# The reciprocals of a Sinkhorn iteration made by GpSimd, as powers of minus one, instead of by VectorE

## The chip, the cores and the metric

One core of one Trainium2 chip runs the kernel. The metric is the device time of one launch in microseconds (us). Three runs of the kernel before gave 2599.68, 2599.71 and 2604.77 us; the median is 2599.71.

## What is computed

The input `x` has 16 batches of 256 tokens by 2048 numbers. Each batch goes through a linear attention (with keys and values from a context of the same shape) and then through a mixing block. The mixing block works per token on four streams of 512 numbers and needs a doubly stochastic 4x4 matrix for every token, which 50 rounds of Sinkhorn normalisation make:

```python
def step(carry, _):
    u, v = carry
    u = -jax.nn.logsumexp(Z + v[..., None, :], axis=-1)
    v = -jax.nn.logsumexp(Z + u[..., :, None], axis=-2)
    return ((u, v), None)
(u, v), _ = jax.lax.scan(step, (u0, v0), None, length=num_iters)   # 50
return jnp.exp(Z + u[..., :, None] + v[..., None, :])
...
x = x + attention(layernorm(x), ctx_4096, ctx_4096, ...)
x = x + mix(layernorm(x), ...)     # H_res = sinkhorn_log(...) in it
```

## The kernel before

Everything runs in f32. For each of the 16 batches the kernel walks a list of **places**: 16 "A" places and 16 "B" places (key logits, their exponentials, the key-value context), and 27 "Q" places (query logits, softmax, attention out, the return of the rows). Each of the five engines has its own program, which walks the same list in order and issues its share of a place, in a fixed order, with semaphore waits. So the order on each engine is written out by hand, and no scheduler changes it.

**The Q places.** Query tiles are handled in pairs, one pair in two places. For a pair VectorE subtracts the maxima (L943, L953), ScalarE takes exponentials (L1260), GpSimd adds the halves of each head (L1501, `query_half`), VectorE sums and inverts (L961, L965, `query_sum`), GpSimd multiplies (L1509, `query_normalise`). Some places later, VectorE floors a norm (L973), GpSimd raises it to the power -0.5 (L1519), VectorE scales the attention output (L983, `scale_pair`), and GpSimd adds it to the rows (L1526, `add_pair`). GpSimd also makes the low halves of the next context (L1480) and of x (L1484), and weight matrices for the mixing (L1491).

**The Sinkhorn iteration.** The 4x4 matrices of several batches are worked on together. `GROUPS = (4, 4, 4, 2, 2)` gives the batches of each of five groups; a batch has two tiles of 128 tokens, so T, the tiles of a group, is 8, 8, 8, 4 and 4. Each round is run as scalings of a matrix `skp`: a **step** is a product with the last scale (L1062 or L1058, 128 x 16T), a sum over rows or columns (L1063 or L1059, 16T to 4T numbers) and a reciprocal (L1064 or L1060, 128 x 4T). After at most 10 rounds ScalarE's logarithms refresh u and v. There are 98 such steps with a reciprocal in a group, among 116 pieces in all. Each of VectorE's small instructions waits for the one before it through `s_skd` (`step`).

The pieces are laid over the places of the batches that follow the group. A batch has 31 places that may take pieces: 16 among the A and B places, and Q5 to Q19. The first two groups have four batches to do it in, so one piece a place. Groups 2 (T = 8) and 3 (T = 4) have two batches each, so nearly every place takes two pieces. The last group, T = 4, is run in the tail, after the last batch. VectorE's and ScalarE's programs each keep a generator (`sinkhorn`) that goes one piece further at each "sink" task.

Of the kernel before, what the change touches and what calls it, by code (L numbers as in the profile page):

```python
# [5 lines left out]
ALU = mybir.AluOpType  # L6
# [30 lines left out]
def xattn_ffn(nc, x, ctx, ctx_t, x_t, wq_t, wk_t, wv_t, wo_t, bo, g, w_maps_t, base, gate, w_branch, streams, coef_rows, bias_rows, out):  # L37
# [212 lines left out]
    with stack:  # L250
        def sb(name, shape, dt=F32):
            return stack.enter_context(nc.sbuf_tensor(name, shape, dt))

        def sem(name):
            return stack.enter_context(nc.semaphore(name))
# [167 lines left out]
        def wait_read(w, n):  # L423
# [6 lines left out]

        SK_ACTS = 5 + 3 * -(-(SINKHORN_ITERS - 1) // REFRESH) + 1
        CONSTS = 11
        SK_STEPS = 3 + 1 + 4 + 1 + 3 + sum(
            6 * min(REFRESH, SINKHORN_ITERS - d) - 1 + 4 for d in range(1, SINKHORN_ITERS, REFRESH)) + 6 + 5

        def sync_program(e):
# [77 lines left out]
            def store_coefs(gr):  # L514
                tokens = slice(FIRST[gr] * C, (FIRST[gr] + GROUPS[gr]) * C)
                T = GROUPS[gr] * CT
                w.wait_ge(s_skd, (gr + 1) * SK_STEPS)
                if gr:
                    for i in range(2):
                        w.wait_ge(s_coef[i], gr * 16)  # L520
                nc.sync.dma_start(coef_rows[tokens].rearrange("(t p) s i -> p t s i", p=P), coef_all[:, 0:T]).then_inc(
                    s_coef[0], 16)
                nc.sync.dma_start(bias_rows[tokens].rearrange("(t p) i -> p t i", p=P), bias_all[:, 0:T]).then_inc(
                    s_coef[1], 16)
# [285 lines left out]
        def vector_program(e):  # L810
# [184 lines left out]
            def step(instruction):  # L995

                instruction.then_inc(s_skd, 1)
                skd[0] += 1
                w.wait_ge(s_skd, skd[0])

            def sinkhorn(gr):
# [9 lines left out]
                def over_j(v):  # L1011
                    return v.unsqueeze(2).broadcast_to([P, T, STREAMS, STREAMS])
# [7 lines left out]
                def over_streams(v):  # L1020
                    return v.unsqueeze(2).broadcast_to([P, T, STREAMS])

                w.wait_ge(s_lg, first + GROUPS[gr])
                if gr:
                    for i in range(2):
# [27 lines left out]
                while done < SINKHORN_ITERS:  # L1053
                    w.wait_ge(s_ska, acts)
                    rounds = min(REFRESH, SINKHORN_ITERS - done)
                    for r in range(rounds):
                        if r:
                            step(nc.vector.tensor_tensor(skw, skp, over_j(skb), ALU.mult))  # L1058
                        step(nc.vector.tensor_reduce(skr, skw if r else skp, AX_X, ALU.add))  # L1059
                        step(nc.vector.reciprocal(ska, skr))  # L1060
                        yield
                        step(nc.vector.tensor_tensor(skw, skp, over_i(ska), ALU.mult))  # L1062
                        step(nc.vector.tensor_reduce(skr, by_column(skw), AX_X, ALU.add))  # L1063
                        step(nc.vector.reciprocal(skb, skr))  # L1064
                        yield
                    done += rounds
                    w.wait_ge(s_ska, acts + 1)
                    step(nc.vector.tensor_tensor(sku, sku, skr, ALU.add))
                    yield
                    w.wait_ge(s_ska, acts + 2)  # L1070
                    step(nc.vector.tensor_tensor(skv, skv, skr, ALU.add))
                    step(nc.vector.tensor_tensor(skw, skz, over_i(sku), ALU.add))
                    step(nc.vector.tensor_tensor(skw, skw, over_j(skv), ALU.add))
                    yield
                    acts += 3
# [161 lines left out]
        def scalar_program(e):  # L1237
# [86 lines left out]

            def own_first(k):
                ct, i = k // STREAMS, k % STREAMS
                w.wait_ge(s_skd, len(GROUPS) * SK_STEPS)
                nc.scalar.activation(own[k], x_sb[(NB - 1) % 2][:, ct, quarter(0)], ACT.Identity,
                                     bias=bias_all[:, own_tile + ct, i:i + 1],
                                     scale=coef_all[:, own_tile + ct, 0, i:i + 1]).then_inc(s_first, 1)  # L1330

            def sinkhorn(gr):
                T = GROUPS[gr] * CT
                skp, skw, ska, skb, skr = (a[:, 0:T] for a in (skp_all, skw_all, ska_all, skb_all, skr_all))
                post = coef_all[:, 0:T, STREAMS, :]

                def function(target, source, func, count):
                    w.wait_ge(s_skd, count)
                    nc.scalar.activation(target, source, func).then_inc(s_ska, 1)

                d = gr * SK_STEPS + 3
# [12 lines left out]
                function(skp, skw, ACT.Exp, d)  # L1354
                yield
                done = 1
                while done < SINKHORN_ITERS:
                    rounds = min(REFRESH, SINKHORN_ITERS - done)
                    done += rounds
                    d += 6 * rounds - 1  # L1360
                    for _ in range(2 * rounds - 1):
                        yield
                    function(skr, ska, ACT.Ln, d)
# [83 lines left out]
        def pool_program(e):  # L1447
# [10 lines left out]
            nc.gpsimd.memset(chain_t, 1.0).then_inc(s_const, 1)  # L1458
            w.wait_ge(s_const, 6)
            nc.gpsimd.memset(half_power[:], -0.5).then_inc(s_const, 1)  # L1460
            w.wait_ge(s_const, 7)

            nc.gpsimd.memset(mix_mask[:], 1.0).then_inc(s_const, 1)
# [57 lines left out]
            def add_pair(b, p):  # L1521
# [110 lines left out]
```

## Time and profile before

| | |
|---|---|
| median of three runs | 2599.71 us |
| the profiled execution's own time | 2600.5 us |
| its span, first to last instruction | 2598.8 us |
| TensorE matmul busy | 2422.8 us (93%) |
| VectorE busy | 1764.0 us (68%) |
| ScalarE busy | 1168.1 us (45%) |
| GpSimd busy | 1068.3 us (41%) |

The busy times are sums over the whole span; a matmul's end is modelled, so 93% says that TensorE had work issued nearly always, not that it ran at its peak. The time of the launch is 1.7 us more than the span. Batches 1 to 3 have no Sinkhorn pieces in them, batches 4 to 11 have one in each of their 31 places, batches 12 to 15 two. From batch 7 on, most batches also carry matmuls of the mixing of finished groups.

### The profile page before, as it was taken

The page shows a single profiled execution, that of the slowest core. Times are in us where ns is not written, and L with a number is a line of the kernel's source. Part 1 is how long each engine was busy: PE and PEld are TensorE (multiplying, and loading weights), DVE is VectorE, ACT ScalarE, POOL GpSimd, SP SyncE. Part 2 cuts the span into 40 slices and gives each one's busy share as a digit, 9 for nine tenths or more (in the row PEclk, how much of TensorE's full clock was granted, in tenths as well). Part 3 has the DMA queues.
Part 4 walks back from the last instruction along what each step waited for, and adds up shares of the span by engine and source line. Part 5 has one row for each costly group of instructions (what it writes and reads, how often), then busy time and mean ns, then how long its engine had stood idle before and what let it go on. Part 6 is the DMA issues. An engine that isn't in the chain of part 4 may idle for free.

```text
span 2598.8 us, 35329 instructions
## 1 busy us (share of the span) xinstructions
PE 2422.8 (93%) x12004; PEld 1920.9 (74%) x12004; DVE 1764.0 (68%) x4242; ACT 1168.1 (45%) x2439; POOL 1068.3 (41%) x979
## 2 busy tenths in 40 slices
PE   7999999999999999999999999999999999999864
PEld 6887878787888787777877778777776776777521
DVE  3554645456877777666766768776688786967787
ACT  3454444445453444446454444535445344443332
POOL 1534536271635345362634527262362442624410
PEclk9999999999999999999999999999999999999877
DMA  7112222313123122225334330323424423331265
GB/s 234 49 66 98 73 91 71 99 40 100 60 67 101 57 98 74 89 72 156 98 122 138 97 125 33 105 75 112 127 65 123 132 84 116 98 117 45 80 184 164
DMA packets 200145, 255.72 MB, mean 98 GB/s; under 512 B 43550, under 2 KB 109854, under 8 KB 199966
## 3 DMA queue, kind: packets, MB, share of 16 engines
q1 hardware_dynamic: 199966, 253.47, 31.1%
q8 instruction: 96, 1.57, 0.3%
q14 instruction: 83, 0.68, 0.1%
HBM read 177.53 MB, written 75.89 MB: 98 GB/s over the span
## 4 chain that ended last, share of the span: by engine, by line
PE 64%; DVE 21%; POOL 6%; issue 6%; ACT 3%; DMA 1%; SPq 0%; DVEq 0%; POOLq 0%; ACTq 0%
PE kc_bank L641 15%; PE big L700 10%; PE tb L742 4%; PE big L615 4%; PE tb L627 4%; PE big L617 3%; PE big L616 3%; PE tb L756 3%; PE big L674 3%; PE big L676 3%; PE big L675 3%; PE tb L685 2%; PE misc L722 2%; DVE stats L883 2%; POOL x_tr L1526 2%
## 5 line engine op out<-in xcount | busy, mean ns | idle before, releaser
L1255 ACT COPY turned<-tb 128x512 f32<-128x512 f32 x512 | 298.7, 587 | 754.4 <-PE tb L685 481.6
L700 PE MATMUL big<-merged,turned 128*128 128x256 f32 x2048 | 494.6, 385 | 32.8 <-ACT turned L1255 26.0
L641 PE MATMUL kc_bank<-ctxt,turned 128*128 128x256 f32 x2048 | 480.7, 381 | 0.0
L700 PEld LDWEIGHTS big<-merged,turned 128*128 128x128 f32 x2048 | 386.2, 191 | 107.9 <-ACT turned L1255 22.5
L641 PEld LDWEIGHTS kc_bank<-ctxt,turned 128*128 128x128 f32 x2048 | 376.0, 191 | 53.4 <-issue 10.8
L1484 POOL TENSOR_TENSOR in_l<-x_sb,in_h 128x512 fp32r<-128x512 f32 x128 | 168.7, 1344 | 589.8 <-ACT in_h L1295 589.8
L1509 POOL TENSOR_TENSOR q_sb<-q_sb,qsum 128x1024 f32<-128x1024 f32 x128 | 243.8, 1905 | 281.6 <-DVE qsum L965 281.5
L674 PE MATMUL big<-wq_h,in_h 128*128 128x512 f32 x512 | 238.3, 465 | 16.9 <-DVE q_sb L953 16.4
L856 DVE TENSOR_REDUCE kmax<-big 128x1 f32<-128x512 f32 x256 | 172.3, 685 | 106.3 <-PE big L617 103.5
L615 PE MATMUL big<-in_h,wk_h 128*128 128x512 f32 x512 | 238.0, 465 | 6.4 <-ACT k_exp L1246 6.1
L756 PE MATMUL tb<-mix_ld,mix_w 121*96 121x512 f32 (+2 forms) x324 | 188.9, 680 | 56.4 <-DVE mix_w L1134 26.3
L943 DVE TENSOR_REDUCE qmax<-big 128x8 f32<-128x512 f32 x256 | 175.9, 687 | 86.8 <-PE big L676 82.8
L617 PE MATMUL big<-in_h,wk_l 128*128 128x512 f32 x512 | 203.7, 398 | 0.0
L616 PE MATMUL big<-in_l,wk_h 128*128 128x512 f32 x512 | 203.4, 397 | 0.0
L676 PE MATMUL big<-wq_h,in_l 128*128 128x512 f32 x512 | 203.1, 397 | 0.0
L675 PE MATMUL big<-wq_l,in_h 128*128 128x512 f32 x512 | 202.8, 396 | 0.0
L1246 ACT ACTIVATE k_exp<-big,kmax 128x512 f32<-128x512 f32 x256 | 175.3, 689 | 49.8 <-DVE kmax L863 49.6
L1501 POOL TENSOR_TENSOR x_pre<-q_sb 128x512 f32<-128x512 f32 x128 | 162.8, 1272 | 76.3 <-ACT q_sb L1260 76.2
L1323 ACT COPY mix_out<-tb 96x512 f32<-96x512 f32 (+2 forms) x162 | 93.9, 580 | 219.5 <-PE tb L756 192.5
L973 DVE TENSOR_SCALAR nrm<-nrm 128x2 f32<-128x2 f32 x128 | 111.4, 870 | 104.4 <-ACT squares L1271 104.0
L1260 ACT ACTIVATE q_sb<-q_sb 128x1024 f32<-128x1024 f32 x128 | 135.6, 1060 | 103.3 <-DVE q_sb L953 103.3
L878 DVE TENSOR_SCALAR on<-kc_bank,ksum 128x256 f32<-128x256 f32 x64 | 31.0, 484 | 222.3 <-PE kc_bank L641 219.8
(148 smaller groups left out, 4490.0 us busy)
## 6 DMA issues: line engine op xcount, KB each, us to landing
mix_ld<-streams SPq DMA_DIRECT2D x157, 240.0 KB
ctxt<-in_ctx_t SPq DMA_DIRECT2D x64, 512.0 KB, 4.3
x_sb<-in_x SPq DMA_DIRECT2D x64, 512.0 KB, 6.2
x_tr<-in_x_t SPq DMA_DIRECT2D x64, 512.0 KB, 6.7
streams<-x_sb SPq DMA_DIRECT2D x64, 512.0 KB, 3.1
stage<-in_ctx SPq DMA_DIRECT2D x60, 512.0 KB, 4.1
out<-mix_out SPq DMA_DIRECT2D x157, 192.0 KB, 2.2
streams<-y_sb SPq DMA_DIRECT2D x32, 256.0 KB, 2.0
```

The lines of the kernel that those rows point to most:

```text
L615: nc.tensor.matmul(big[i], wk_h[:, ct, cols], in_h[:, ct, quarter(i)], start=ct == 0, stop=False)
L616: nc.tensor.matmul(big[i], wk_h[:, ct, cols], in_l[:, ct, quarter(i)], start=False, stop=False)
L617: t = nc.tensor.matmul(big[i], wk_l[:, ct, cols], in_h[:, ct, quarter(i)], start=False, stop=ct == CT - 1)
L641: t = nc.tensor.matmul(kc_bank[:, 0:C], turned[n % 3][:, j * P:(j + 1) * P], ctxt[:, nt, :], start=nt == 0, stop=nt == NT - 1)
L674: nc.tensor.matmul(big[i % 2], in_h[:, ct, at], wq_h[:, ct, :], start=ct == 0, stop=False)
L675: nc.tensor.matmul(big[i % 2], in_h[:, ct, at], wq_l[:, ct, :], start=False, stop=False)
L676: t = nc.tensor.matmul(big[i % 2], in_l[:, ct, at], wq_h[:, ct, :], start=False, stop=ct == CT - 1)
L700: t = nc.tensor.matmul(big[2 + p % 2][:, half], turned[n % 3][:, dt * P:(dt + 1) * P], merged[:, dt, :], start=dt == 0, stop=dt == DT - 1)
L756: t = nc.tensor.matmul(bank[0:count * STREAMS, :], weights, mix_ld[k][0:ONES + 1, :], start=True, stop=True)
L943: nc.vector.tensor_reduce(qmax[:, i % 2, :], big[i % 2].rearrange(heads, d=DIM_HEAD), AX_X, ALU.max).then_inc(s_qmax, 1)
L1255: nc.scalar.copy(turned[k % 3][:], tb[n % 2][:]).then_inc(s_tba, 1)
L1509: nc.gpsimd.tensor_tensor(exps, exps, qsum[:, p % 2, 1, :].unsqueeze(2).broadcast_to([P, 2 * HEADS, DIM_HEAD]), ALU.mult).then_inc(s_qn, 1)
```

## The change

For all groups but the last, VectorE's reciprocal of each step is dropped. GpSimd's program gets a generator of its own which, at the same "sink" task, waits for the sum (`s_skd`) and writes `skr ** -1` as a TENSOR_TENSOR of 128 x 4T with the operation `pow` and a tile of minus ones; `s_ski` counts these. VectorE's next product waits for `s_ski`, and so does ScalarE's logarithm at a refresh. The counts of `s_skd` are adapted everywhere (`sk_steps`).

```diff
+                def reciprocal(target):
+
+                    if gr == LAST:
+                        step(nc.vector.reciprocal(target, skr))
+
+                def inverted():
+                    if gr < LAST:
+                        halves[0] += 1
+                        w.wait_ge(s_ski, halves[0])
+
...
                         if r:
+                            inverted()
                             step(nc.vector.tensor_tensor(skw, skp, over_j(skb), ALU.mult))
                         step(nc.vector.tensor_reduce(skr, skw if r else skp, AX_X, ALU.add))
-                        step(nc.vector.reciprocal(ska, skr))
+                        reciprocal(ska)
                         yield
+                        inverted()
                         step(nc.vector.tensor_tensor(skw, skp, over_i(ska), ALU.mult))
                         step(nc.vector.tensor_reduce(skr, by_column(skw), AX_X, ALU.add))
-                        step(nc.vector.reciprocal(skb, skr))
+                        reciprocal(skb)
                         yield
...
+            def sinkhorn(gr):
+                T = GROUPS[gr] * CT
+                ska, skb, skr = (a[:, 0:T] for a in (ska_all, skb_all, skr_all))
+                w.wait_ge(s_minus, 1)
+                for _ in range(5):
+                    yield
+                d = sum(map(sk_steps, range(gr))) + 12
+                done = 1
+                while done < SINKHORN_ITERS:
+                    rounds = min(REFRESH, SINKHORN_ITERS - done)
+                    done += rounds
+                    for r in range(rounds):
+                        d += 2 if r else 1
+                        w.wait_ge(s_skd, d)
+                        nc.gpsimd.tensor_tensor(ska, skr, minus_one[:, 0:T], ALU.pow).then_inc(s_ski, 1)
+                        yield
+                        d += 2
+                        w.wait_ge(s_skd, d)
+                        nc.gpsimd.tensor_tensor(skb, skr, minus_one[:, 0:T], ALU.pow).then_inc(s_ski, 1)
+                        yield
+                    d += 4
+                    yield
+                    yield
+
             def behind(place):
                 for task in tasks.get(place, ()):
                     b = task[1]
+                    if task[0] == "sink" and b < LAST:
+                        if b not in running:
+                            running[b] = sinkhorn(b)
+                        next(running[b], None)
```

What stands on GpSimd in two Q places of a batch of group 0, before (L1519 the power of the norm, L1501 the half sums, L1509 the normalisation, L1526 the rows):

```order
L1519 TENSOR_TENSOR nrm<-nrm,half_power 128x2
L1501 TENSOR_TENSOR x_pre<-q_sb 128x512
L1509 TENSOR_TENSOR q_sb<-q_sb,qsum 128x1024
L1526 TENSOR_TENSOR x_tr<-x_tr,on 128x512
L1480 TENSOR_TENSOR in_l<-stage,in_h 128x512
L1519 TENSOR_TENSOR nrm<-nrm,half_power 128x2
```

And in the same places after the change (the same four are L1547, L1529, L1537 and L1554 there, the context's low half is L1508, and L1570 and L1574 are the new powers):

```order
L1547 TENSOR_TENSOR nrm<-nrm,half_power 128x2
L1529 TENSOR_TENSOR x_pre<-q_sb 128x512
L1570 TENSOR_TENSOR ska<-skr,minus_one 128x32
L1537 TENSOR_TENSOR q_sb<-q_sb,qsum 128x1024
L1554 TENSOR_TENSOR x_tr<-x_tr,on 128x512
L1508 TENSOR_TENSOR in_l<-stage,in_h 128x512
L1574 TENSOR_TENSOR skb<-skr,minus_one 128x32
L1547 TENSOR_TENSOR nrm<-nrm,half_power 128x2
```

One power stands ahead of the normalisation, the other between the rows' addition and the power of the norm.

On VectorE in the same two places, before (L1062 and L1063, L1058 and L1059 are a step's product and sum):

```order
L943 TENSOR_REDUCE qmax<-big 128x8
L961 TENSOR_REDUCE qsum<-x_pre 128x16
L965 RECIPROCAL qsum<-qsum 128x16
L953 TENSOR_TENSOR q_sb<-big,qmax 128x512
L973 TENSOR_SCALAR nrm<-nrm 128x2
L1062 TENSOR_TENSOR skw<-skp,ska 128x128
L1063 TENSOR_REDUCE skr<-skw 128x32
L1064 RECIPROCAL skb<-skr 128x32
L943 TENSOR_REDUCE qmax<-big 128x8
L953 TENSOR_TENSOR q_sb<-big,qmax 128x512
L983 SCALAR_TENSOR_TENSOR on<-big,nrm,g_rows 128x256 x2
L1058 TENSOR_TENSOR skw<-skp,skb 128x128
```

And after (L952, L970, L974, L962, L982, L992 are the query's instructions, L1085 and L1086, L1080 and L1081 the steps'):

```order
L952 TENSOR_REDUCE qmax<-big 128x8
L970 TENSOR_REDUCE qsum<-x_pre 128x16
L974 RECIPROCAL qsum<-qsum 128x16
L962 TENSOR_TENSOR q_sb<-big,qmax 128x512
L982 TENSOR_SCALAR nrm<-nrm 128x2
L1085 TENSOR_TENSOR skw<-skp,ska 128x128
L1086 TENSOR_REDUCE skr<-skw 128x32
L952 TENSOR_REDUCE qmax<-big 128x8
L962 TENSOR_TENSOR q_sb<-big,qmax 128x512
L992 SCALAR_TENSOR_TENSOR on<-big,nrm,g_rows 128x256 x2
L1080 TENSOR_TENSOR skw<-skp,skb 128x128
L1081 TENSOR_REDUCE skr<-skw 128x32
```

Only the reciprocal of the step is gone; all else keeps its place. In a batch of group 2, with two pieces a place, two powers stand together on GpSimd after the change:

```order
L1537 TENSOR_TENSOR q_sb<-q_sb,qsum 128x1024
L1554 TENSOR_TENSOR x_tr<-x_tr,on 128x512
L1508 TENSOR_TENSOR in_l<-stage,in_h 128x512
L1574 TENSOR_TENSOR skb<-skr,minus_one 128x32
L1570 TENSOR_TENSOR ska<-skr,minus_one 128x32
L1547 TENSOR_TENSOR nrm<-nrm,half_power 128x2
L1529 TENSOR_TENSOR x_pre<-q_sb 128x512
L1508 TENSOR_TENSOR in_l<-stage,in_h 128x512
L1574 TENSOR_TENSOR skb<-skr,minus_one 128x32
L1570 TENSOR_TENSOR ska<-skr,minus_one 128x32
```

Before, the same stretch had none of the L1570 and L1574 rows; the second of two waits for VectorE's product and sum, which wait for the first.

## Rows read from the trace of the kernel before

**Rows 1.** The page's first part: busy time, share of span, instructions.

```profile
PE 2422.8 (93%) x12004; PEld 1920.9 (74%) x12004; DVE 1764.0 (68%) x4242; ACT 1168.1 (45%) x2439; POOL 1068.3 (41%) x979
```

**Rows 2.** Busy time by stretch: batch 1, batch 5, batch 12, the tail.

```profile
181.13:322.06 140.93, 138.17 (x731) 115.53 (x730) 73.84 (x159) 65.57 (x135) 63.99 (x51) 1.00 0.24 79
748.49:892.91 144.42, 139.23 (x730) 115.41 (x729) 107.30 (x249) 66.32 (x138) 64.00 (x52) 1.00 0.23 77
1801.93:1974.85 172.92, 159.68 (x765) 123.08 (x763) 135.83 (x326) 75.99 (x159) 69.16 (x69) 0.98 0.35 108
2457.04:2598.80 141.76, 78.33 (x124) 21.93 (x124) 108.53 (x392) 42.59 (x87) 15.05 (x41) 0.75 0.61 172
```

**Rows 3.** Timeline of GpSimd in batch 5: start us, duration us, instruction [idle before].

```profile
823.18 1.91 POOL L1509 TENSOR_TENSOR q_sb<-q_sb,qsum 128x1024 f32<-128x1024 f32 x1 [2.64 <-DVE qsum L965]
825.05 1.41 POOL L1526 TENSOR_TENSOR x_tr<-x_tr,on 128x512 f32<-128x512 f32 x1
826.42 1.27 POOL L1480 TENSOR_TENSOR in_l<-stage,in_h 128x512 fp32r<-128x512 f32 x1
827.65 0.70 POOL L1519 TENSOR_TENSOR nrm<-nrm,half_power 128x2 f32<-128x2 f32 x1
...
832.23 1.91 POOL L1509 TENSOR_TENSOR q_sb<-q_sb,qsum 128x1024 f32<-128x1024 f32 x1 [1.34 <-DVE qsum L965]
...
840.02 1.90 POOL L1509 TENSOR_TENSOR q_sb<-q_sb,qsum 128x1024 f32<-128x1024 f32 x1 [2.63 <-DVE qsum L965]
```

**Rows 4.** Timeline of VectorE in the same two places.

```profile
828.38 0.88 DVE L983 SCALAR_TENSOR_TENSOR on<-big,nrm,g_rows 128x256 f32<-128x256 f32 x2 [0.92 <-POOL nrm L1519]
829.18 0.56 DVE L1062 TENSOR_TENSOR skw<-skp,ska 128x128 f32<-128x128 f32 x1
829.77 0.39 DVE L1063 TENSOR_REDUCE skr<-skw 128x32 f32<-128x128 f32 x1
830.19 0.35 DVE L1064 RECIPROCAL skb<-skr 128x32 f32<-128x32 f32 x1
830.58 0.69 DVE L943 TENSOR_REDUCE qmax<-big 128x8 f32<-128x512 f32 x1
831.19 0.68 DVE L961 TENSOR_REDUCE qsum<-x_pre 128x16 f32<-128x512 f32 x1
831.90 0.25 DVE L965 RECIPROCAL qsum<-qsum 128x16 f32<-128x16 f32 x1
```

**Rows 5.** Groups of instructions by form: busy us, mean ns of one.

```profile
L1060 DVE RECIPROCAL ska<-skr 128x32 f32<-128x32 f32 x147 | 51.9, 353 | 5.1
...
L1501 POOL TENSOR_TENSOR x_pre<-q_sb 128x512 f32<-128x512 f32 x128 | 162.8, 1272 | 76.3 <-ACT q_sb L1260 76.2
L1519 POOL TENSOR_TENSOR nrm<-nrm,half_power 128x2 f32<-128x2 f32 x128 | 89.8, 701 | 66.7 <-DVE nrm L973 64.3
L1491 POOL TENSOR_TENSOR mix_w<-mix_mask,mix_co 120x96 f32<-120x96 f32 x151 | 53.8, 364 | 100.2 <-DMA mix_w<-bias_rows 100.2
```

**Rows 6.** Timeline of VectorE among the B places of batch 5.

```profile
750.29 0.29 DVE L1059 TENSOR_REDUCE skr<-skw 128x32 f32<-128x128 f32 x1
...
761.06 0.35 DVE L1060 RECIPROCAL ska<-skr 128x32 f32<-128x32 f32 x1
763.24 0.48 DVE L878 TENSOR_SCALAR on<-kc_bank,ksum 128x256 f32<-128x256 f32 x1 [1.83 <-PE kc_bank L641]
...
768.60 0.41 DVE L845 COPY on<-tb 128x256 f32<-128x256 f32 x1
...
771.89 0.69 DVE L856 TENSOR_REDUCE kmax<-big 128x1 f32<-128x512 f32 x1
...
782.13 0.35 DVE L1064 RECIPROCAL skb<-skr 128x32 f32<-128x32 f32 x1
```

**Rows 7.** Timeline of GpSimd in batch 12 (group 2) and batch 14 (group 3).

```profile
1895.06 1.90 POOL L1509 TENSOR_TENSOR q_sb<-q_sb,qsum 128x1024 f32<-128x1024 f32 x1 [6.45 <-DVE qsum L965]
...
1905.33 1.91 POOL L1509 TENSOR_TENSOR q_sb<-q_sb,qsum 128x1024 f32<-128x1024 f32 x1 [2.54 <-DVE qsum L965]
...
2234.87 1.91 POOL L1509 TENSOR_TENSOR q_sb<-q_sb,qsum 128x1024 f32<-128x1024 f32 x1 [3.26 <-DVE qsum L965]
...
2244.75 1.91 POOL L1509 TENSOR_TENSOR q_sb<-q_sb,qsum 128x1024 f32<-128x1024 f32 x1 [2.00 <-DVE qsum L965]
```

More of the change, by code:

```diff
@@ L317, in xattn_ffn @@
         s_skd = sem("s_skd")
+        s_minus = sem("s_minus")
+        s_ski = sem("s_ski")
         s_ska = sem("s_ska")
@@ L367, in xattn_ffn @@
         half_power = sb("half_power", [P, CT])
+        minus_one = sb("minus_one", [P, TMAX, STREAMS])
         neg_m2 = sb("neg_m2", [P, CT])
@@ L432, in xattn_ffn, with sk_steps @@
         CONSTS = 11
+        HALVES = 2 * (SINKHORN_ITERS - 1)
+        def sk_steps(gr):
+            return SK_STEPS - (HALVES if gr < LAST else 0)
         SK_STEPS = 3 + 1 + 4 + 1 + 3 + sum(
@@ L516, in store_coefs @@
                 T = GROUPS[gr] * CT
-                w.wait_ge(s_skd, (gr + 1) * SK_STEPS)
+                w.wait_ge(s_skd, sum(map(sk_steps, range(gr + 1))))
                 if gr:
@@ L1021, in over_streams @@
                     return v.unsqueeze(2).broadcast_to([P, T, STREAMS])
+                halves = [gr * HALVES]
+                def reciprocal(target):
[5 more added lines that the diff above has]
+                        w.wait_ge(s_ski, halves[0])
                 w.wait_ge(s_lg, first + GROUPS[gr])
@@ L1057, in sinkhorn @@
                         if r:
+                            inverted()
                             step(nc.vector.tensor_tensor(skw, skp, over_j(skb), ALU.mult))
                         step(nc.vector.tensor_reduce(skr, skw if r else skp, AX_X, ALU.add))
-                        step(nc.vector.reciprocal(ska, skr))
+                        reciprocal(ska)
                         yield
+                        inverted()
                         step(nc.vector.tensor_tensor(skw, skp, over_i(ska), ALU.mult))
                         step(nc.vector.tensor_reduce(skr, by_column(skw), AX_X, ALU.add))
-                        step(nc.vector.reciprocal(skb, skr))
+                        reciprocal(skb)
                         yield
                     done += rounds
+                    inverted()
                     w.wait_ge(s_ska, acts + 1)
@@ L1326, in own_first @@
                 ct, i = k // STREAMS, k % STREAMS
-                w.wait_ge(s_skd, len(GROUPS) * SK_STEPS)
+                w.wait_ge(s_skd, sum(map(sk_steps, range(len(GROUPS)))))
                 nc.scalar.activation(own[k], x_sb[(NB - 1) % 2][:, ct, quarter(0)], ACT.Identity,
@@ L1339, in function @@
                     nc.scalar.activation(target, source, func).then_inc(s_ska, 1)
-                d = gr * SK_STEPS + 3
+                d = sum(map(sk_steps, range(gr))) + 3
                 function(skp, skp, ACT.Exp, d)
@@ L1355, in sinkhorn @@
                 yield
-                done = 1
+                done, halves = 1, gr * HALVES
                 while done < SINKHORN_ITERS:
@@ L1359, in sinkhorn @@
                     done += rounds
-                    d += 6 * rounds - 1
+                    d += (6 if gr == LAST else 4) * rounds - 1
                     for _ in range(2 * rounds - 1):
                         yield
+                    if gr < LAST:
+                        halves += 2 * rounds
+                        w.wait_ge(s_ski, halves)
                     function(skr, ska, ACT.Ln, d)
@@ L1460, in pool_program @@
             nc.gpsimd.memset(half_power[:], -0.5).then_inc(s_const, 1)
+            nc.gpsimd.memset(minus_one[:], -1.0).then_inc(s_minus, 1)
             w.wait_ge(s_const, 7)
@@ L1526, in add_pair @@
                 nc.gpsimd.tensor_tensor(pair, pair, on[:], ALU.add).then_inc(s_sum, 1)
+            def sinkhorn(gr):
[21 more added lines that the diff above has]
+                    yield
+            running = {}
             def behind(place):
```

## The prediction

> **What bounds the kernel now.** I read the page's busy shares first, then the busy times of stretches, then the timelines of GpSimd and VectorE side by side, and last the groups by form for prices.
>
> The shares suggest room: GpSimd is busy 41% of the span, VectorE 68% [rows 1]. The stretches say how little VectorE's load costs. A batch without Sinkhorn pieces takes 140.93 us, with TensorE busy for 138.17; batch 5, with one piece a place, takes 144.42 although VectorE is busy 33 us more [rows 2]. So in the batches of groups 0 and 1 all the pieces together cost about 3.5 us a batch. Batch 12, with two pieces a place and mixing matmuls as well, takes 172.92.
>
> Where those few us go is seen in the timelines. Through the Q places runs a ring between GpSimd and VectorE. GpSimd normalises (L1509, 1.91), adds rows (L1526, 1.41), in every second pair makes a context half (L1480, 1.27), takes the power of the norm (L1519, 0.70) [rows 3]; VectorE waited 0.92 for exactly that power, scales (L983, 0.88), does the step (0.56, 0.39, 0.35), then L943, L961 and L965 (0.69, 0.68, 0.25) [rows 4], and L965 releases the next L1509. The sum is 9.1 us, and the ring took 9.05 (823.18 to 832.23); the next one, without a context half, took 7.79 (832.23 to 840.02) [rows 3]. The mean is 8.4. GpSimd's 41% is thus misleading: in the Q places it is half of what sets the pace.
>
> **The change part by part.** *Removed:* 3 x 98 reciprocals of 128x32 at 353 ns and 98 of 128x16. A step on VectorE goes from one start to the next in 0.39 us for the reciprocal (830.19 to 830.58 [rows 4]). Of a pair's two, one is in the ring; the other stands beside GpSimd's normalisation.
>
> *Added:* 392 powers on GpSimd. Their price, W, is the large unknown. The trace has powers of 128x2 only, 701 ns. GpSimd's products and sums take 1272 ns for 512 elements and 364 for 96 [rows 5], so 2.2 ns an element on a base of 0.155 us. Of the power's 0.70 us some 0.54 are therefore its own arithmetic, for two elements. If all of it is start-up, a 128x32 costs 0.70 + 30 x 0.0022 = 0.77 us and a 128x16 0.73. If all of it is paid per element (0.27 each), they cost 0.155 + 32 x 0.272 = 8.9 and 4.5 us. No row lies between. [...] Between ends a factor of twelve apart I take the geometric middle, 2.6 us for 128x32 and 1.8 for 128x16, and keep both ends.
>
> The Trainium skill, "GPSIMD Engine Reference", section 4.1, says to do elementwise work on VectorE, GpSimd being about 2x slower, and section 3.1 gives about 2.6 cycles per element for a two-input operation. By that count, as an estimate from the page, 30 more elements would add 0.065 us and the power would be at my lower end, with the sum at about 2677 us. The trace agrees for products (2.2 ns an element); for powers it shows only that two elements already cost far more than that [rows 5].
>
> *Ring, one piece a place.* By the order in the section on the change, the power of the odd place stands between the rows' addition and the power of the norm, so all of W enters the ring; the power of the even place runs beside L943, L961 and L965, which give 1.6 us of cover, and only W - 1.6 shows. With about 0.1 us for two handovers a pair becomes longer by W + 0.1 - 0.39 + max(0, W - 1.6): 0.48 us at the low end, 3.3 at 2.6, 15.9 at the high end. Of a batch's 31 places 15 are Q places; 98 of 116 pieces carry a power; that is 22 pairs a group, 44 for groups 0 and 1. Sum: +21, +146, +700 us. Queued behind the power on GpSimd are L1519 and the next L1509; VectorE's scaling waits for the one, TensorE's transposes for the other, so nothing hides it.
>
> *A and B places, one piece.* Here GpSimd is mostly idle. The 16 steps run from 750.29 to 782.48, 32.2 us or 2.0 each [rows 6]. After the change a step cannot repeat sooner than product and sum (0.67) + two handovers (0.17) + W: 1.6 us at the low end, 3.4 in the middle, 9.7 at the high. At the low end only the four steps that follow at 1.07 us in each run of B places get longer, partly in the idle 1.83 us in front of L878: I take +9 us in all. Otherwise 16 steps take 55 or 156 us instead of 32, so 1.43 or 7.7 us a step, for 2 x 54 steps: +154, +834.
>
> *Groups 2 and 3, two pieces a place.* Both powers of a place are in the chain, since the second waits for a product and a sum that wait for the first. The ring becomes 1.9 + 1.4 + 0.64 (half of L1480) + 0.7 + 0.87 + three times 0.67 + 0.5 of handovers = 8.0, + 3W + max(W, 1.6): 11.9, 18.4, 43.6 us, against 10.27 before [rows 7]. There are 11 such pairs in group 2: +18, +89, +366. In group 3 the steps are smaller (0.5), the base 7.5 and the powers 128x16: 11.3, 14.7, 25.5 against 9.88 [rows 7], +15, +53, +172. In their 27 A and B places with powers a place becomes two steps, one exposed power with its handovers, and the longer of the second power and 1.1 to 1.2 us of VectorE's other work (L856 0.69 and a chain instruction, as L845 0.41 [rows 6]): for T = 8 it goes from 3.3 (two steps of 1.07 and the other work) to 3.5, 6.9, 19.5 us (+5, +97, +437), for T = 4 from 2.8 to 3.1, 4.9, 10.3 (+8, +57, +203).
>
> *The rest:* the last group is as before; ScalarE's logarithms wait for `s_ski` where they waited for the reciprocal, within the W counted; one memset more at the start is hidden behind the first loads. Nothing moves on TensorE or the DMA queues.
>
> **The sum.** Low 21+9+18+15+5+8 = 76; middle 146+154+89+53+97+57 = 596; high 700+834+366+172+437+203 = 2712. On the profiled execution's 2600.5 us that is 2677, 3197 and 5312; the median of the runs stands 0.8 below that execution, which changes nothing here.
>
> **The rivals.**
> *A, the power is nearly all start-up* (W up to about 1.3 us): 2677 to 2830 us. For it: a product costs hardly more for more elements. Against: 0.54 us for two elements is long for a mere start.
> *B, the power is paid element by element* (W of 6 us and more for 128x32): 4300 to 5312 us. For it: the arithmetic must be done on every element, and nothing in the trace shows that it overlaps. Against: only that GpSimd's simple loop does overlap its elements.
> *C, VectorE's relief wins* (the other side). If W with its handovers were below 0.39 us, the ring and the two-piece places would only lose reciprocals: 44 x 0.39 = 17 us in the first ring, about 1.5 us for each of 22 pairs (33) and 0.7 us for each of 54 A and B places (38): 2600 - 88 = 2512 us. Against it stands the row of 128x2, already at 0.70 [rows 5]; it decides only below W = 0.3.
> *D, GpSimd's power fits everywhere in idle time*, since it is busy only 41%: then no change, 2600. Against: the ring, in which VectorE already waits for GpSimd [rows 4].
> One thing may add to the middle case: in the tail, where TensorE is busy 78.33 of 141.76 us, its granted clock is 0.75 [rows 2], a mix of its two levels (1.2 and 2.4 GHz). If TensorE waits for the ring and its clock falls for stretches of the batches, its 138 us of work a batch at 2.4 GHz would become the bound again. I don't add it; the range covers it.
>
> **How the numbers follow.** Middle, W from 1.3 to 6 us: chance 0.50, own range 2830 to 4300, time 3200. B 0.26; A 0.18; C 0.03; D 0.03. The range of 8 in 10 leaves out the edges of A and B, so 2690 to 5300; it is wide because one price is unknown by a factor of twelve and enters 392 times. A measurement of this kernel can tell about 0.2% from no change. Faster by more than that is C, 0.03; within it D, 0.03; slower 0.94.
>
> **What would show it.** In the profile after: the two lines of powers with their mean for 128x32 and 128x16 (W itself; the whole size of the result hangs on it); VectorE's products waiting for them; GpSimd's L1509 rows of batch 5 more than 8.4 us apart, at about 11.7 for W = 2.6; batches 1 to 3 still at 140.9 us and the tail of the last group unchanged. Per power, groups 2 and 3 should lose more than groups 0 and 1 at the same W. It would be wrong in mechanism if the powers are long and the batches keep their length, or if the lost time stands in front of instructions that neither GpSimd nor VectorE releases; wrong in size if W is far from 2.6.

## The result

| | before | after |
|---|---|---|
| median | 2599.69 us (4 runs, 2599.59 to 2604.77) | 4045.94 us (4 runs, 4045.14 to 4047.53) |
| ratio | | 1.555, interval 1.553 to 1.557 |

The kernel got slower by 1446 us. The forecast was slower, 3200 us, in a range of 2690 to 5300: the side and the range held, but the loss was 2.4 times the 596 us that the sum had. The range held because it was wide: it ran from a power of under 1 us to one of 8.9 us.

The page after begins so (shares of the span in brackets, against [rows 1]):

```profile
span 4044.5 us, 35511 instructions
...
PE 2801.9 (69%) x12004; PEld 2154.8 (53%) x12004; DVE 1700.6 (42%) x3850; ACT 1165.6 (29%) x2439; POOL 2926.7 (72%) x1372
```

VectorE's busy time fell by 63 us, although the 392 reciprocals that it no longer makes had taken 129 (353 and 253 ns each): the products of the steps (L1080 and L1085, before L1058 and L1062), which now often start beside a GpSimd product, took 295 us in all against 173, as the last section explains, and the scalar operation on the norm (L982, before L973) 55 against 111. GpSimd's busy time grew by 1858 us. The groups of GpSimd's instructions by form name the price (busy us, mean ns of one):

```profile
L1574 POOL TENSOR_TENSOR skb<-skr,minus_one 128x32 f32<-128x32 f32 x147 | 798.0, 5429 | 111.0 <-DVE skr L1086 111.0
L1570 POOL TENSOR_TENSOR ska<-skr,minus_one 128x32 f32<-128x32 f32 x147 | 798.0, 5429 | 143.2 <-DVE skr L1081 143.2
...
L1570 POOL TENSOR_TENSOR ska<-skr,minus_one 128x16 f32<-128x16 f32 x49 | 142.2, 2902 | 40.4 <-DVE skr L1081 40.4
...
L1547 POOL TENSOR_TENSOR nrm<-nrm,half_power 128x2 f32<-128x2 f32 x128 | 89.8, 702 | 46.6 <-DVE nrm L982 44.5
```

The three sizes lie on one line: 0.375 us and 0.158 us an element give 0.69, 2.90 and 5.43 us. A 128x32 power took 5.43 us where I had taken 2.6, between ends of 0.77 and 8.9.

The chain of work that ended last changed hands. The page before and the page after have, as shares of the span:

```profile
PE 64%; DVE 21%; POOL 6%; issue 6%; ACT 3%; DMA 1%; SPq 0%; DVEq 0%; POOLq 0%; ACTq 0%
POOL 53%; PE 25%; DVE 14%; issue 6%; ACT 2%; DMA 0%; SPq 0%; DVEq 0%; POOLq 0%; ACTq 0%
```

From batch 4 to batch 15, where the powers are, the chain after goes over the powers L1570 and L1574 for 1720 of 3299 us and over TensorE for 443.

By stretch the loss sits where the forecast put it (batches 1, 5, 12, 14; against [rows 2]):

```profile
180.34:321.24 140.90, 138.15 (x731) 115.54 (x730) 73.83 (x159) 65.51 (x135) 64.08 (x51) 1.00 0.24 79
858.03:1120.63 262.60, 170.22 (x730) 134.98 (x728) 106.30 (x219) 65.96 (x138) 219.38 (x81) 0.81 0.13 42
2578.90:3001.39 422.49, 210.25 (x775) 155.64 (x774) 122.05 (x275) 76.75 (x160) 355.18 (x121) 0.71 0.15 45
3381.17:3663.76 282.59, 187.69 (x768) 140.81 (x767) 112.59 (x277) 76.48 (x159) 223.82 (x123) 0.82 0.22 70
```

Batch 1, without Sinkhorn pieces, is where it was (140.90 against 140.93). Batch 5 went from 144.4 to 262.6, batch 12 from 172.9 to 422.5. The tail with the last group takes 142.1 us (3902.37 to the end) against 141.8.

The ring in the Q places of group 0, on GpSimd's timeline (start, duration; against [rows 3]):

```profile
733.76 1.90 POOL L1537 TENSOR_TENSOR q_sb<-q_sb,qsum 128x1024 f32<-128x1024 f32 x1
735.62 1.31 POOL L1554 TENSOR_TENSOR x_tr<-x_tr,on 128x512 f32<-128x512 f32 x1
736.89 1.27 POOL L1508 TENSOR_TENSOR in_l<-stage,in_h 128x512 fp32r<-128x512 f32 x1
738.11 5.44 POOL L1574 TENSOR_TENSOR skb<-skr,minus_one 128x32 f32<-128x32 f32 x1
743.52 0.69 POOL L1547 TENSOR_TENSOR nrm<-nrm,half_power 128x2 f32<-128x2 f32 x1
744.18 1.25 POOL L1529 TENSOR_TENSOR x_pre<-q_sb 128x512 f32<-128x512 f32 x1
745.39 1.31 POOL L1508 TENSOR_TENSOR in_l<-stage,in_h 128x512 fp32r<-128x512 f32 x1
746.67 5.43 POOL L1570 TENSOR_TENSOR ska<-skr,minus_one 128x32 f32<-128x32 f32 x1
752.07 1.90 POOL L1537 TENSOR_TENSOR q_sb<-q_sb,qsum 128x1024 f32<-128x1024 f32 x1
...
763.07 5.44 POOL L1570 TENSOR_TENSOR ska<-skr,minus_one 128x32 f32<-128x32 f32 x1 [0.55 <-DVE skr L1081]
768.48 1.90 POOL L1537 TENSOR_TENSOR q_sb<-q_sb,qsum 128x1024 f32<-128x1024 f32 x1
```

GpSimd has no gap from 733.76 to 752.07: in the pair with context halves its own queue sets the time. In the next pair it waits once, 0.55 us for VectorE's sum at 763.07. A pair takes 18.31 us with context halves and 16.41 without, 17.36 in the mean; 8.4 plus the prediction's W + 0.1 - 0.39 + (W - 1.6) at W = 5.43 is 17.4. On VectorE's timeline of the same places the waits stand in brackets:

```profile
733.82 1.98 DVE L1085 TENSOR_TENSOR skw<-skp,ska 128x128 f32<-128x128 f32 x1 [3.33 <-POOL ska L1570]
...
744.25 0.88 DVE L992 SCALAR_TENSOR_TENSOR on<-big,nrm,g_rows 128x256 f32<-128x256 f32 x2 [6.58 <-POOL nrm L1547]
...
747.97 0.15 DVE L982 TENSOR_SCALAR nrm<-nrm 128x2 f32<-128x2 f32 x1
752.13 1.99 DVE L1085 TENSOR_TENSOR skw<-skp,ska 128x128 f32<-128x128 f32 x1 [4.01 <-POOL ska L1570]
```

The longest wait is not for the reciprocal itself but for the power of the norm (L1547), queued behind a power of the iteration. Among the A and B places GpSimd's powers follow one another with little between them but the handovers and VectorE's product and sum:

```profile
859.52 5.43 POOL L1570 TENSOR_TENSOR ska<-skr,minus_one 128x32 f32<-128x32 f32 x1 [0.80 <-DVE skr L1081]
865.76 5.43 POOL L1574 TENSOR_TENSOR skb<-skr,minus_one 128x32 f32<-128x32 f32 x1 [0.81 <-DVE skr L1086]
871.91 5.43 POOL L1570 TENSOR_TENSOR ska<-skr,minus_one 128x32 f32<-128x32 f32 x1 [0.73 <-DVE skr L1081]
```

That is 6.2 us a step; the formula's 0.67 + 0.17 + W is 6.27. From 908 us on in the same batch a GpSimd product (L1512) runs between the powers, VectorE's product beside it takes 1.3 us, and a step takes 7.2. And with two pieces a place (batch 12) both powers are exposed:

```profile
2774.03 5.43 POOL L1570 TENSOR_TENSOR ska<-skr,minus_one 128x32 f32<-128x32 f32 x1 [0.79 <-DVE skr L1081]
2779.43 1.90 POOL L1537 TENSOR_TENSOR q_sb<-q_sb,qsum 128x1024 f32<-128x1024 f32 x1
2781.96 5.42 POOL L1574 TENSOR_TENSOR skb<-skr,minus_one 128x32 f32<-128x32 f32 x1 [0.64 <-DVE skr L1086]
2788.18 5.42 POOL L1570 TENSOR_TENSOR ska<-skr,minus_one 128x32 f32<-128x32 f32 x1 [0.79 <-DVE skr L1081]
2793.57 0.69 POOL L1547 TENSOR_TENSOR nrm<-nrm,half_power 128x2 f32<-128x2 f32 x1
...
2808.05 1.95 POOL L1537 TENSOR_TENSOR q_sb<-q_sb,qsum 128x1024 f32<-128x1024 f32 x1
```

From 2779.43 to 2808.05 the pair takes 28.6 us; the formula 8.0 + 4W gives 29.7.

### The profile page after: what moved, and what is told of

Same layout as the page of the kernel before. It is cut to its first block, busy times and chain, and to the rows that moved or that the text cites. A ratio compares the mean times of both kernels' runs of the same rounds, so it can differ in the third digit from the quotient of the medians.

```text
span 4044.5 us, 35511 instructions
## 1 busy us (share of the span) xinstructions
PE 2801.9 (69%) x12004; PEld 2154.8 (53%) x12004; DVE 1700.6 (42%) x3850; ACT 1165.6 (29%) x2439; POOL 2926.7 (72%) x1372
## 4 chain that ended last, share of the span: by engine, by line
POOL 53%; PE 25%; DVE 14%; issue 6%; ACT 2%; DMA 0%; SPq 0%; DVEq 0%; POOLq 0%; ACTq 0%
POOL skb L1574 22%; POOL ska L1570 21%; PE kc_bank L650 6%; PE big L709 4%; POOL q_sb L1537 3%; DVE skw L1085 2%; DVE skw L1080 2%; PE big L624 2%; POOL x_pre L1529 2%; POOL x_tr L1554 2%; POOL in_l L1508 2%; PE big L626 2%; PE big L625 2%; DVE skr L1086 1%; DVE stats L892 1%
## 5 line engine op out<-in xcount | busy, mean ns | idle before, releaser
L1570 POOL TENSOR_TENSOR ska<-skr,minus_one 128x32 f32<-128x32 f32 (+1 forms) x196 | 940.2, 4797 | 183.7 <-DVE skr L1081 183.7
L1574 POOL TENSOR_TENSOR skb<-skr,minus_one 128x32 f32<-128x32 f32 (+1 forms) x196 | 940.2, 4797 | 138.3 <-DVE skr L1086 138.3
L709 PE MATMUL big<-merged,turned 128*128 128x256 f32 x2048 | 594.7, 442 | 276.8 <-DVE on L992 220.3
L709 PEld LDWEIGHTS big<-merged,turned 128*128 128x128 f32 x2048 | 445.5, 222 | 396.0 <-DVE on L992 274.6
L650 PE MATMUL kc_bank<-ctxt,turned 128*128 128x256 f32 x2048 | 539.6, 415 | 2.3 <-ACT turned L1279 2.3
L1085 DVE TENSOR_TENSOR skw<-skp,ska 128x128 f32<-128x128 f32 (+1 forms) x245 | 160.6, 656 | 665.4 <-POOL ska L1570 663.8
L1080 DVE TENSOR_TENSOR skw<-skp,skb 128x128 f32<-128x128 f32 (+1 forms) x220 | 134.7, 612 | 603.8 <-POOL skb L1574 602.2
L1537 POOL TENSOR_TENSOR q_sb<-q_sb,qsum 128x1024 f32<-128x1024 f32 x128 | 243.6, 1903 | 148.3 <-DVE qsum L974 148.3
L992 DVE SCALAR_TENSOR_TENSOR on<-big,nrm,g_rows 128x256 f32<-128x256 f32 x256 | 111.9, 479 | 400.6 <-POOL nrm L1547 400.2
L1512 POOL TENSOR_TENSOR in_l<-x_sb,in_h 128x512 fp32r<-128x512 f32 x128 | 164.5, 1298 | 147.7 <-ACT in_h L1319 147.7
L636 PE MATMUL tb<-ident,k_exp 128*128 128x128 f32 x1024 | 173.5, 299 | 119.6 <-DVE merged L861 70.3
L636 PEld LDWEIGHTS tb<-ident,k_exp 128*128 128x128 f32 x1024 | 140.3, 155 | 170.3 <-DVE merged L861 79.4
```

What stands on the lines that cost most here:

```text
L636: t = nc.tensor.transpose(bank[:, j * P:(j + 1) * P], k_exp[:, at:at + P], ident[:])
L650: t = nc.tensor.matmul(kc_bank[:, 0:C], turned[n % 3][:, j * P:(j + 1) * P], ctxt[:, nt, :], start=nt == 0, stop=nt == NT - 1)
L709: t = nc.tensor.matmul(big[2 + p % 2][:, half], turned[n % 3][:, dt * P:(dt + 1) * P], merged[:, dt, :], start=dt == 0, stop=dt == DT - 1)
L1537: nc.gpsimd.tensor_tensor(exps, exps, qsum[:, p % 2, 1, :].unsqueeze(2).broadcast_to([P, 2 * HEADS, DIM_HEAD]), ALU.mult).then_inc(s_qn, 1)
L1570: nc.gpsimd.tensor_tensor(ska, skr, minus_one[:, 0:T], ALU.pow).then_inc(s_ski, 1)
L1574: nc.gpsimd.tensor_tensor(skb, skr, minus_one[:, 0:T], ALU.pow).then_inc(s_ski, 1)
```

## The experiments

The theory after the result: the forecast's chains are right, and the whole loss is the price of a power, which grows with its elements, put into them. Rivals: the handovers and GpSimd's fixed order cost by themselves; the powers were long only because two engines got in each other's way; TensorE's lower granted clock (0.824 over the span) made up a part.

**e1_sizes: the disputed price alone.**

```diff
+            timed(nc.gpsimd.memset(base_t, 3.7))
+            timed(nc.gpsimd.memset(exp_t, -1.0))
+            timed(nc.gpsimd.memset(half_t, -0.5))
+            for size in (1, 2, 4, 8, 16, 32, 64, 128):
+                timed(nc.gpsimd.tensor_tensor(out_t[:, 0:size], base_t[:, 0:size], exp_t[:, 0:size], ALU.pow))
+            for size in (2, 32):
+                timed(nc.gpsimd.tensor_tensor(out_t[:, 0:size], base_t[:, 0:size], half_t[:, 0:size], ALU.pow))
+            for size in (2, 16, 32, 128):
+                timed(nc.gpsimd.tensor_tensor(out_t[:, 0:size], base_t[:, 0:size], exp_t[:, 0:size], ALU.mult))
```

> The kernel before, with a list of single GpSimd instructions ahead of its work, each alone and waited for: powers with exponent -1 of 128 x 1, 2, 4, 8, 16, 32, 64 and 128 elements, powers with exponent -0.5 of 2 and 32, products of 2, 16, 32 and 128. Theory (the price is the power's own arithmetic, paid per element): from the 5.43 us at 32 and 2.90 us at 16 of the changed kernel, 0.375 us + 0.158 us an element: 0.53, 0.69, 1.0, 1.6, 2.9, 5.4, 10.5, 20.6 us, the exponent without influence, products 0.16, 0.19, 0.23, 0.44 us. Rival (in the changed kernel the powers were long because VectorE's and GpSimd's accesses get in each other's way): alone, the power of 32 takes well under 4 us. The launch gets at most 45 us longer.

Measured, groups by form of the first 60 us (busy us, mean ns):

```profile
L1489 POOL TENSOR_TENSOR y_sb<-x_pre,pre_t 128x128 f32<-128x128 f32 x1 | 20.8, 20779 | 0.1
L1489 POOL TENSOR_TENSOR y_sb<-x_pre,pre_t 128x64 f32<-128x64 f32 x1 | 10.5, 10545 | 0.1
L1489 POOL TENSOR_TENSOR y_sb<-x_pre,pre_t 128x32 f32<-128x32 f32 x1 | 5.4, 5426 | 0.1
L1491 POOL TENSOR_TENSOR y_sb<-x_pre 128x32 f32<-128x32 f32 x1 | 5.4, 5426 | 0.1
L1489 POOL TENSOR_TENSOR y_sb<-x_pre,pre_t 128x16 f32<-128x16 f32 x1 | 3.5, 3458 | 0.1
L1489 POOL TENSOR_TENSOR y_sb<-x_pre,pre_t 128x8 f32<-128x8 f32 x1 | 1.7, 1686 | 0.1
L1489 POOL TENSOR_TENSOR y_sb<-x_pre,pre_t 128x4 f32<-128x4 f32 x1 | 1.5, 1521 | 0.1
L1489 POOL TENSOR_TENSOR y_sb<-x_pre,pre_t 128x2 f32<-128x2 f32 x1 | 0.7, 709 | 0.1
...
L1493 POOL TENSOR_TENSOR y_sb<-x_pre,pre_t 128x128 f32<-128x128 f32 x1 | 0.5, 453 | 0.1
L1493 POOL TENSOR_TENSOR y_sb<-x_pre,pre_t 128x32 f32<-128x32 f32 x1 | 0.3, 252 | 0.1
```

Alone, a power of 128x32 takes 5.426 us as in the loaded kernel, with either exponent. From 32 to 64 and to 128 elements it rises by 0.160 us an element. So the price is the power's own, and interference plays no part in it. A product of the same size takes 0.25 us, a twentieth. The powers of 4 and of 16 elements are about 0.5 us over the line of the changed kernel in this one run; the launch took 2613.64 us, 13 more than the kernel before.

**e2_product: all the waits, a cheap operation.** The reciprocals are left out of the computation: every scale is one.

```diff
-            nc.gpsimd.memset(minus_one[:], -1.0).then_inc(s_minus, 1)
+            nc.gpsimd.memset(minus_one[:], 1.0).then_inc(s_minus, 1)
...
-nc.gpsimd.tensor_tensor(ska, skr, minus_one[:, 0:T], ALU.pow).then_inc(s_ski, 1)
+nc.gpsimd.tensor_tensor(ska, minus_one[:, 0:T], minus_one[:, 0:T], ALU.mult).then_inc(s_ski, 1)
```

> The changed kernel with all its waits and its order, but each power is replaced by a product of the tile of ones with itself, of the same 128 x 4T form (so the reciprocals are left out of the computation). Theory (the price of the power makes the loss): the product costs 0.23 us, less than the 0.39 us that VectorE saves; ring 8.4 - 0.39 + 0.1 + 0.23, places with two pieces about as before: 2585 to 2605 us. Rival (the handovers between the engines and GpSimd's fixed order cost by themselves, whatever the operation): 2650 us or more.

Measured: 2592.56 us, ratio 0.9966 (0.9953 to 0.9978). The products took 238 ns for 128x32. The rival that order and handovers cost by themselves is out. It says more: even with an instruction of 0.24 us in its place, taking 392 reciprocals off VectorE brings 8 us. In the profiled executions batches 4 to 11 got 9.7 us shorter and batches 12 to 15, with two pieces a place, 4.2 us longer.

**e3_groups01 and e4_groups23: each half of the change alone.** The conditions `gr < LAST` become `gr in POWERED`, with `POWERED = (0, 1)` and `(2, 3)`.

> The change for groups 0 and 1 alone (one piece a place). Theory with W = 5.43 us in the formulas of the prediction: 44 pairs at +9.0 us and 108 steps at +4.3 us, 855 us: 3455 us; by the lengths of batches 4 to 11 in the changed kernel (+778) 3378 us. Rival (TensorE's lower clock makes up a good part, and only where all groups are changed): less than 3300 us, and this excess and that of the other half don't add up to 1446.

> The change for groups 2 and 3 alone (two pieces a place). Theory: 213 + 249 for group 2 at W = 5.43 us, 101 + 117 for group 3 at 2.90 us, 680 us: 3280 us, with GpSimd's normalisations of batch 12 about 30 us apart. Per power that is 3.5 us against 4.0 in groups 0 and 1, since half of its powers are of half the size. Rival (two powers in a place overlap with each other or with other work): under 3150 us.

Measured: 3382.72 and 3270.32 us. Over the 2600.9 us of the kernel before on that chip these are +781.9 and +669.5, together 1451, against 1446 for the whole change. So the losses add up, and no effect that needs the whole change is left. This says nothing on TensorE's clock, which falls in each half by itself: it is 0.80 in batch 5 of e3 and 0.71 in batch 12 of e4, as in the whole change (0.81 and 0.71). The price is the same when a half stands alone:

```profile
L1571 POOL TENSOR_TENSOR ska<-skr,minus_one 128x32 f32<-128x32 f32 x98 | 532.1, 5430 | 106.1 <-DVE skr L1082 106.1
```

**e6_half: about half the price.** GpSimd makes the power for half of the columns, VectorE the reciprocal for the others.

```diff
+                    half = T // 2 if gr < LAST else 0
+                    step(nc.vector.reciprocal(target[:, half:T], skr[:, half:T]))
...
+nc.gpsimd.tensor_tensor(ska[:, 0:T // 2], skr[:, 0:T // 2], minus_one[:, 0:T // 2], ALU.pow).then_inc(s_ski, 1)
```

> Each power is made for half of the columns only, and VectorE's reciprocal for the other half stays beside it; the result is the same. W = 2.90 us for 128x16 and about 1.65 for 128x8. Theory: 44 x 4.3 + 108 x 1.7 + 11 x 9.3 + 27 x 4.2 + 11 x 4.2 + 27 x 1.8 = 685 us over the kernel before: 3285 us. Rival (the loss is simply in proportion to the time of the powers, 1013 us here against 1881): 1446 x 1013/1881 = 779, 3380 us; a fixed part of the loss would give still more.

Measured: 3215.54 us, 615 over before. The powers took 2.903 us (128x16) and 1.639 (128x8):

```profile
L1570 POOL TENSOR_TENSOR ska<-skr,minus_one 128x16 f32<-128x16 f32 x147 | 426.7, 2903 | 144.1 <-DVE skr L1081 144.1
```

The formulas gave 685, proportion to the powers' time 779. The formulas are nearer, and 70 too high. By the lengths of the batches all of that is in groups 0 and 1, which lost 300 us where the formulas have 373; groups 2 and 3 lost 315, against 311. The run also compares the groups at one price: at 2.9 us a power cost 1.5 us in groups 0 and 1 here and 2.1 in group 3 of the changed kernel, so two powers in a place cost more each, as forecast.

**e5_twice: twice the price.**

```diff
+                def first_power():
+                    nc.gpsimd.tensor_tensor(spare[:, 0:T], skr, minus_one[:, 0:T], ALU.pow).then_inc(s_twice, 1)
+                    twice[0] += 1
+                    w.wait_ge(s_twice, twice[0])
...
+                        first_power()
                         nc.gpsimd.tensor_tensor(ska, skr, minus_one[:, 0:T], ALU.pow).then_inc(s_ski, 1)
```

> The changed kernel with each power made twice, first into a spare tile and then into its own, the second waiting for the first: W = 10.9 us for T = 8, 5.85 for T = 4. Theory (formulas of the prediction, W entering the ring once, the even places beyond 1.6 us, the other places in full): 44 x 19.8 + 108 x 9.7 + 11 x 41 + 27 x 20 + 11 x 20.9 + 27 x 10.1 = 3420 us over the kernel before: 6020 us; GpSimd's normalisations of batch 5 about 28.4 us apart in the mean. Rival (part of the loss of the changed kernel is a fixed cost, such as the slower clock of a waiting TensorE, which is paid already): the same excess again would not come; under 5700 us.

Measured: 5901.57 us, 3301 over before, 1856 over the changed kernel. Twice the price cost 2.28 times as much, as a chain does that has used up its cover. The rival of a fixed part, under 5700, is out. The terms of the expectation add up to 3412 rather than 3420, which changes nothing. GpSimd's normalisations are 29.31 and 27.40 us apart, 28.4 in the mean as expected:

```profile
809.92 1.90 POOL L1539 TENSOR_TENSOR q_sb<-q_sb,qsum 128x1024 f32<-128x1024 f32 x1
839.23 1.90 POOL L1539 TENSOR_TENSOR q_sb<-q_sb,qsum 128x1024 f32<-128x1024 f32 x1
866.63 1.90 POOL L1539 TENSOR_TENSOR q_sb<-q_sb,qsum 128x1024 f32<-128x1024 f32 x1
```

**f1_step_first and f2_step_first_g01: shortening the ring of the kernel before.** If the ring is real, a step that stands in VectorE's wait for the norm should leave it.

```diff
+                    early = i >= 8 and i % 2 == 0 and ahead(place)
                     if i >= 8 and i % 2 == 0 and i < NT + 8:
                         scale_pair(b, (i - 8) // 2)
...
-                    behind(place)
+                    behind(place, early)
```

`ahead` makes the place's first piece, and `behind` then leaves that piece out. f2 does so for groups 0 and 1 only.

> The kernel before, with one thing moved: in the even Q places VectorE makes the (first) piece of the iteration ahead of scaling the pair (L983), instead of behind it. Theory (the ring): in pairs with a context half VectorE waits 0.9 us for GpSimd's power of the norm and the step of 1.05 us fits there, so those pairs go from 9.05 to about 7.9 us, the others from 7.8 to 7.9: 0.5 us for each of about 50 pairs of groups 0 and 1, 25 us, 2575 us. Rival (the step's product is held up by GpSimd's running instruction, and the scaling with it): no change or slower, 2600 to 2620 us. In the two-piece places VectorE waits for nothing, so nothing should come there.

> As f1_step_first, but only for groups 0 and 1. Theory: the same gain, 2575 us; if the two-piece places lose by the earlier step (GpSimd's addition of rows and the return of the pair come 1.05 us later, while nobody waited), f2 is faster than f1 by up to 20 us. Rival: no gain in either.

Measured: f1 2602.13 us, ratio 1.000 (0.9991 to 1.0009); f2 2595.46 us, ratio 0.9981 (0.9972 to 0.9990). The ring did as expected; f2's normalisations in batch 5, where [rows 3] has 9.05 and 7.79 us:

```profile
821.27 1.90 POOL L1523 TENSOR_TENSOR q_sb<-q_sb,qsum 128x1024 f32<-128x1024 f32 x1 [1.61 <-DVE qsum L965]
...
829.20 1.90 POOL L1523 TENSOR_TENSOR q_sb<-q_sb,qsum 128x1024 f32<-128x1024 f32 x1 [0.24 <-DVE qsum L965]
...
836.94 1.90 POOL L1523 TENSOR_TENSOR q_sb<-q_sb,qsum 128x1024 f32<-128x1024 f32 x1 [1.76 <-DVE qsum L965]
```

They are 7.93 and 7.74 apart. But the launch gained 5 us, not 25: by the starts of successive batches, batches 5 and 6 went from 144.4 and 144.8 to 142.4 and 142.2 us, near the 140.9 of a batch with no pieces at all, in which TensorE is busy for 138. The 0.5 us a pair can't all be kept. Batches 4 to 7 gained 4.4 us in f2, and batches 8 to 11, which carry mixing matmuls too, nothing (612.3 against 612.2). In f1, where the two-piece places are changed too, batches 12 and 13 take 176.4 and 173.8 us against 172.9 and 169.1 in f2, which gives the gain back. f2 is the fastest kernel here that computes the reference, 0.2% faster than the kernel before.

## Why the prediction was wrong in size

**The step that failed** is the one on the price: "Between ends a factor of twelve apart I take the geometric middle, 2.6 us for 128x32 and 1.8 for 128x16". It measured 5.43 and 2.90 us. Both ends rested on the one size in the trace, 128x2. The upper one took a product's base of 0.155 us for the power's base too, and so 0.27 us an element; the power's own base is 0.375 us, and 0.158 us an element remains. The lower end supposed that elements cost next to nothing. No row stood behind a size between them. A geometric middle was no estimate of anything: with an operation paid per element it is far too low, and the text had the argument for that in its rival B. The waits, the covers and the paths were not what failed: at the measured price they give the loss to 6%.

**With the measured price in the prediction's own formulas** the terms come out so:

| | forecast | formula at 5.43 and 2.90 us | measured |
|---|---|---|---|
| groups 0 and 1, Q places | 146 | 395 | |
| groups 0 and 1, A and B places | 154 | 460 | |
| groups 0 and 1, both | 300 | 855 | 778 |
| group 2 | 186 | 462 | 459 |
| group 3 | 110 | 218 | 210 |
| sum | 596 | 1535 | 1446 |

Measured is the length of batches 4 to 11, 12 and 13, 14 and 15 (to the last power of a variance, L1591), after less before: 1975.8 - 1198.0, 802.3 - 343.7, 521.2 - 311.4. So the formulas are 6% too high in all, and 2% in groups 2 and 3. The same comparison at three prices, loss in us by the formulas and measured:

| | half (2.90, 1.64 us) | changed kernel | twice |
|---|---|---|---|
| groups 0 and 1 | 373, measured 300 | 855, measured 778 | 1919, measured 1818 |
| groups 2 and 3 | 311, measured 315 | 680, measured 668 | 1494, measured 1483 |

**What the formula still overstates** is in groups 0 and 1, by 73, 77 and 101 us: nearly the same at each price, so it is some idle time that was there before and not the price of an element. By batch, a power cost 4.1 us in batches 4 to 6 (82 powers, 339 us), 3.7 in the last batch of each group (16 powers; batches 7 and 11, 59 us each) and 3.9 in batches 8 to 10 (82 powers, 321 us). Batches 4 to 7 lost 398 us (983.9 - 585.7) and batches 8 to 11 lost 380 (991.9 - 612.2), against 427 each. The latter carry mixing matmuls in their A and B places and were longer before, so a step there may have had more than the 2.0 us of batch 5 to hide in. That is argued from these lengths, not tried, and it would explain only the 18 us between the two; where the rest hides stays open.

**The other points.** *The ring* was right: the order put the odd place's power ahead of the power of the norm, and there VectorE waits 6.58 us. That its length fits so well is partly luck where there are context halves: GpSimd's queue, which the prediction didn't add up, is full there (18.31 us), and the ring would have been 18.0 (9.05 + 8.97). *Two powers in a place both exposed*: right, group 2 lost 4.7 us a power (459 by 98), groups 0 and 1 lost 4.0 at the same price, group 3 with its smaller powers 2.1. *The last group and the batches without pieces unchanged*: right.

*Rival A* (start-up only) is out by e1, *B* (per element) had the right law and the wrong constant: its mark of 6 us for 128x32 was just above the 5.43 measured, which lies near the top of the 1.3 to 6 us that the middle case took for its own. *C* (VectorE's relief wins if W is below 0.3 us) was tried by e2 at 0.24 us: the sign was right, the price of 88 us was not, and 8 came. Of the 88, 71 were for the two-piece places, which gained nothing; in the batches with one piece a place, TensorE's 138 us are close below the 142 to 144 that batches 4 to 6 took. *D*, the power in idle time, is out by the result: in the pair with context halves GpSimd has no idle time left.

*TensorE's clock*: it did fall where TensorE waits (granted 0.81 in batch 5, 0.71 in batch 12), and the matmuls L709 took 442 ns in the mean against 385 before (L700 there). It did not decide. In batch 5 the chain that ended last goes over GpSimd and VectorE for 211 of 262.6 us and over TensorE for 28: 22 us between the A and B places and the Q places with pieces, and 6 us near the end. Some of its matmuls ran at the lower level (granted clock 0.50 from 944 to 952 us, 1.00 from 955 to 959), at twice the time of the others:

```profile
947.96 3.41 PE kc_bank L650 x8
...
955.89 3.47 PE kc_bank L650 x16
```

The pieces at that level sum to some 9 us (4.1 from 947.30, 4.6 from 1088.46), so by an estimate from these rows the lower clock cost 4 to 5 us of the 118 that batch 5 lost. And the formulas, which hold no term for the clock, are not too low where it is lowest (group 2: 462 against 459). Over batches 4 to 15 TensorE has 443 us of the chain; if all of it ran at the lower level, the clock would have made half of that, 222 us, which is an upper bound and not a measurement. The prediction named the clock as an addition to the middle case and added nothing for it; these rows show it small, not nothing.

## What to carry to other kernels

A price read at one size is not a price at another: before an operation that the trace shows for 2 elements is moved in at 32, run it alone at two or three sizes, and until then take the per-element reading as seriously as the start-up one. A busy share of 41% doesn't say that an engine has room; follow who releases whom, and see whether the new instruction lands between two handovers. And before work is taken off an engine, ask for the most it can bring with a stand-in that costs next to nothing: here 8 us.

## What the runs showed of the hardware

A GpSimd power of 128 partitions costs 0.375 us and 0.158 us an element of a partition, from the loaded kernels' 128x2, 128x8, 128x16 and 128x32 (0.70, 1.64, 2.90, 5.43 us). Alone it takes the same at 32 elements with either exponent, and 0.160 us an element from there to 128. A product costs 2 ns an element (252 to 453 ns from 32 to 128 elements). Why the single powers of 4 and 16 elements took about 0.5 us more than that line, while 98 powers of 16 elements in the changed kernel took 2.90, stays open.

A power leaves VectorE alone, a product does not. Before, and after inside a power (896.98 to 902.40):

```profile
823.65 1.46 DVE L973 TENSOR_SCALAR nrm<-nrm 128x2 f32<-128x2 f32 x1
...
897.60 0.75 DVE L1184 SCALAR_TENSOR_TENSOR x_pre<-x_sb,pre,x_pre 128x512 f32<-128x512 f32 x1
```

VectorE's scalar operation on 128x2 (L973 before, L982 after) took 1.46 us at 823.65, beside the normalisation L1509 (823.18 to 825.09), and ended with it; all 52 times that it started during a power of the iteration it took 0.10 to 0.17 us. L1184, which reads two SBUF tiles, took 0.74 to 0.75 us in all 18 single rows inside such a power, as it does with GpSimd idle. And VectorE's 128x128 product L1085 took 1.98 us when it started at 733.82 with GpSimd's normalisation (733.76 to 735.66), 1.3 beside L1512, and 0.28 to 0.29 where no GpSimd instruction ran at its start. The Trainium skill, "SBUF — State Buffer", section "Terms", says that the port pair the two share is locked for the full instruction and that the loser fully blocks. The normalisations agree; for the powers the rows disagree, and the measurement decides: of the 15 kinds of VectorE instruction with ten or more records and some of them begun during powers of the iteration, none took over 0.01 us more than the longest of its kind beside an idle GpSimd. Why is not shown.
